# Section numbers of the graph hops read into registers for two groups at once, on SyncE and VectorE

## What is computed

```python
for _ in range(N_HOPS):            # 3
    h = agg[head]
    t = agg[tail]
    left = h @ q_w
    right = jnp.tanh(rel * t @ k_w)
    att = jnp.sum(left * right, axis=1)
    seg_max = jax.ops.segment_max(att, head, num_segments=n)
    e = jnp.exp(att - seg_max[head])
    seg_sum = jax.ops.segment_sum(e, head, num_segments=n)
    w = e / seg_sum[head]
    msg = w[:, None] * rel * t
    summed = jax.ops.segment_sum(msg, head, num_segments=n)
    agg = summed / jnp.maximum(cnt, 1.0)[:, None]
    norm = jnp.linalg.norm(agg, axis=1, keepdims=True)
    agg = agg / jnp.maximum(norm, 1e-12)
    out = out + agg + entity_emb
```

## Time and profile before

| | us |
|---|---|
| median of 3 timed runs | 11539.55 |
| lowest and highest | 11534.21, 11544.98 |
| span of the profiled execution | 11570.2 |
| PE busy, share of the span | 8077.2, 70% |
| DVE busy | 6642.3, 57% |
| POOL busy | 6401.1, 55% |
| ACT busy | 6199.6, 54% |

### The profile page before, as it was taken

One profiled execution on the slowest core, in us unless ns is written; L12 is line 12 of the kernel. 1 busy time (PEld: TensorE's weight loads), 2 busy tenths in 40 slices (PEclk: granted clock), 3 DMA queues, 4 the chain that ended last, 5 costly groups with the idle time before them and its releaser, 6 DMA issues. The chain is left out here.

```text
span 11570.2 us, 241070 instructions
## 1 busy us (share of the span) xinstructions
PE 8077.2 (70%) x47197; PEld 6146.6 (53%) x47197; DVE 6642.3 (57%) x27980; ACT 6199.6 (54%) x15908; POOL 6401.1 (55%) x6757
## 2 busy tenths in 40 slices
PE   2666666666688888888866666666666666666665
PEld 2444444444466666666645555555554555555554
DVE  4666666665555565655655555555554555555556
ACT  1666666666355555555545555555554555555554
POOL 4566666664455555555545555555545555555553
PEclk8776677767788999999978888888888888888887
DMA  2111111111455555555544444444434444444443
GB/s 68 43 43 43 43 43 42 43 43 41 123 176 176 177 176 176 177 175 176 176 124 139 138 138 138 137 139 136 138 118 134 136 138 137 138 136 136 137 136 112
DMA packets 1180950, 1401.16 MB, mean 121 GB/s; under 512 B 216215, under 2 KB 883640, under 8 KB 1180472
## 3 DMA queue, kind: packets, MB, share of 16 engines
q1 hardware_dynamic: 963734, 951.33, 25.8%
q0 software_dynamic: 216064, 444.28, 14.2%
q10 hardware_dynamic: 876, 2.56, 0.1%
HBM read 888.87 MB, written 183.76 MB: 93 GB/s over the span
## 5 line engine op out<-in xcount | busy, mean ns | idle before, releaser
L622 POOL DMA_INDIRECT tails<-node_rows,idx x4992 | 4715.4, 945 | 3803.9 <-remote 1610.6
L1798 DVE SCALAR_TENSOR_TENSOR acc<-acc,fade,banks 128x129 f32 x4992 | 1741.7, 349 | 2100.6 <-remote 1310.5
L1902 PE MATMUL banks<-rt,weight_t 128*128 128x129 f32 x9984 | 1674.8, 315 | 749.1 <-DVE acc L1798 724.3
L622 POOL DMA_INDIRECT l_rows<-in_x_dram,l_idx x1664 | 1591.9, 957 | 1075.1 <-issue 453.6
L1951 ACT ACTIVATE weight<-att,low 128x128 f32<-128x128 f32 x4992 | 1593.0, 391 | 1058.6 <-DVE low L1822 577.1
L1902 PEld LDWEIGHTS banks<-rt,weight_t 128*128 128x128 f32 x9984 | 1483.3, 223 | 849.8 <-issue 795.8
L1887 PE MATMUL banks<-rtt,k_sb 128*128 128x512 f32 x2496 | 1505.3, 685 | 533.8 <-issue 441.7
L1872 PE MATMUL banks<-right,window 128*128 128x128 f32 x9984 | 1567.3, 307 | 281.8 <-DVE tile_low L1814 163.4
L1814 DVE CUSTOM_DVE_ANT_0 att<-banks,agg 128x128 f32<-128x128 f32 x4992 | 1152.8, 287 | 982.6 <-remote 768.9
L1872 PEld LDWEIGHTS banks<-right,window 128*128 128x128 f32 x9984 | 1430.9, 221 | 358.3 <-DVE tile_low L1814 227.5
L1929 ACT ACTIVATE right<-banks 128x512 f32<-128x512 f32 x1248 | 730.5, 585 | 809.3 <-remote 639.2
(11 more groups left out here) (317 smaller groups left out, 9961.5 us busy)
## 6 DMA issues: line engine op xcount, KB each, us to landing
window<-qt SPq DMA_DIRECT2D x4992, 64.0 KB
agg<-pairs_kept SPq DMA_DIRECT2D x832, 384.0 KB
pairs_kept<-agg SPq DMA_DIRECT2D x416, 384.0 KB
rows_in<-tile_rows SPq DMA_DIRECT2D x208, 512.0 KB
tails<-node_rows,idx POOLq DMA_INDIRECT x4992
l_rows<-in_x_dram,l_idx POOLq DMA_INDIRECT x1664
node_rows<-agg SPq DMA_DIRECT2D x6, 1024.0 KB, 6.0
node_rows<-agg SPq DMA_DIRECT2D x3, 1088.0 KB, 8.2
```

Source lines behind the costliest of these rows:

```text
L622: e.indirect_dma_start(out=rows[:, g, t, :], out_offset=None, in_=of, in_offset=bass.IndirectOffsetOnAxis(ap=idx[:, b, first + t:first + t ...
L1798: e.scalar_tensor_tensor(to, to, fade[:, g2, t:t + 1], bank[b_acc + t // 2][:, t % 2 * WIDE:t % 2 * WIDE + WIDE], ALU.mult, ALU.add).then_ ...
L1902: mm = s.e.matmul(bank[b_acc + t // 2][:, t % 2 * WIDE:t % 2 * WIDE + WIDE], weight_t[:, s.slot(lag, 2), t, :], rt[:, s.slot(lag, RING), t ...
```

## The change

A new helper loads eight numbers at even steps and none at odd ones; a step takes the first or the last four of what is held. Both users in the hops are moved to it: SyncE's for the windows (lag 2) and VectorE's for the updates (lag 7). The calls now stand ahead of the test whether the step has a group at that lag. The first layer keeps the old helper.

```diff
+        def load_two_groups(s, e_type, at_section, most, lag, held):
+            if s.i % 2 == 0:
+                a = max(s.i - lag, 0)
+                b = min(s.i - lag + 2, z.slot_groups) if s.turn is None else s.i - lag + 2
+                if a < b:
+                    held[:] = load_sections(s, e_type, at_section, most, s.i - a, 0, (b - a) * GROUP)
+            if s.live(lag):
+                return held[-GROUP:] if (s.i % 2 or s.i == lag - 1) else held[:GROUP]
...
+                columns_held, wides_held = [], []
...
+                    q = load_two_groups(s, mybir.EngineType.SP, at_column, (z.sections - 1) * P, 2, columns_held)
                     if s.live(2):
                         g4 = s.slot(2, UNROLL)
-                        q = load_sections(s, mybir.EngineType.SP, at_column, (z.sections - 1) * P, 2)
                         s.wait_ge((s_att, done(2 + UNROLL)))
...
                 def update(s, lag):
+                    q = load_two_groups(s, mybir.EngineType.DVE, at_wide, (z.sections - 1) * WIDE, lag, wides_held)
                     if s.live(lag):
                         e, g2 = s.e, s.slot(lag, 2)
-                        q = load_sections(s, mybir.EngineType.DVE, at_wide, (z.sections - 1) * WIDE, lag)
                         s.wait_ge((s_acc, done(lag)), (s_taken, done(lag + 1, GROUP)))
```

## The result

| | before, us | after, us | ratio, 95% interval |
|---|---|---|---|
| median of 4 timed runs | 11538.52 | 11463.14 | 0.9935 (0.9921 to 0.9949) |
| span of the profiled execution | 11570.2 | 11460.8 | |

The change made the kernel 75 us faster, 0.65%. Forecast were 250 us, in a range that ended at 11080 and 11550. The time lies in the range and on the forecast side, but the gain is less than a third of the forecast.

A forecast was written before the change was run, and what follows sets the result against it. SyncE was taken to set the hops' pace; 0.43 - 0.03 = 0.40 us saved in two steps, 0.20 a group, times 1248 groups = 250 us. 11570 - 250 = 11320, less 30 for the timed median: 11290, range 11080 to 11550.

The forecast's parts named there:

- SyncE, even steps: SyncE's load of eight numbers instead of four in the hops: 0.03 us more; upper bound a 1402 ns load.
- What bounds the kernel: In the hops SyncE, waiting for nobody while others wait for its DMAs, sets the pace: 6.65 us a group.
- So no second engine cuts the gain short: In the hops, GpSimd's 5.0 and VectorE's 3.5 us a group stay under the 6.45 us left, so nothing limits the gain.
- SyncE, odd steps: In SyncE's odd hop steps one load and its address instruction go, with two joints: 0.43 us saved.
- VectorE: VectorE's loads before its updates in the hops: counted as nothing, with 0 to 100 us from hop 1 kept in the range.
- C: Rival: all engines' instruction total sets the pace; 1.0% fewer give about 120 us, 11420; chance 0.17.
- D: Rival: no change; SyncE's hold-ups are a matter of time or DMAs and fill the freed 0.20 us, 11540; chance 0.14.
- B: Rival: SyncE's hold-ups shrink with its fewer instructions, 470 us gained, 11070; chance 0.14.
- E: Rival: slower, SyncE's load of eight is dear; at 1402 ns it costs 420 us, 11960; chance 0.07.
- some 60 us if eight cost as much as two fours: By the Trainium skill's 200 ns a register, only the address instruction with its joint is saved, 0.09 us in two steps.
- What would show it: Signs in the profile after: fewer loads, medians near 330 and 400 ns, shorter hops, SyncE's own waits staying near nothing.
- A: The forecast case: SyncE's free duration comes back in the hops, 250 us gained, 11290; chance 0.48.

The follow-up runs named there:

- sp_no_load_again: Kernel before, but SyncE keeps the first group's four numbers for a whole hop, on a chip with hold-ups: 69 us faster, ratio 0.9950.
- vector_only: The change on VectorE alone against the kernel before; SyncE loads four numbers in every step as before: 11698.48 us, ratio 0.9999.
- sizes: Kernel before, but SyncE's load of section numbers has another size in each of 8 loop steps: 8906.64 us beside 8889.67.
- sp_no_load: Kernel before, but SyncE keeps the first group's four numbers for a whole hop, on the chip without hold-ups: 8887.8 us beside 8889.67, ratio 0.9998.

## Why the prediction was off

Two steps failed: the price of the load of eight, and the check for what is late next.

*SyncE, even steps*, 0.03 us more for eight numbers: measured 0.23 (525 against 297 ns). It was a line drawn through one number and four, and both lie on one step of the staircase. The upper bound, 1402 ns, held the value; the choice was by a slope where the nearest rows could not tell a slope from a step. With 0.23 the sum becomes 125 us, so this term is 125 of the 175 us by which the forecast was too high.

*What bounds the kernel.* "An engine that waits for nobody while others wait for its DMAs is the one that sets the pace" was right, but only for the next 70 to 100 us. SyncE was indeed the first limit with hold-ups: its part alone gave the whole gain, and ScalarE's wait for it fell by 731 us. The step that failed is the sentence "So no second engine cuts the gain short". It compared a group's 6.45 us with the gathers' 5.0 and VectorE's busy 3.5 us, that is with the work of engines that are not held up. Held up are their chains too, and the earlier trace rows showed VectorE's update standing 7.85 us, and the earlier trace rows 1310.5 us of such waits, more than ScalarE's 1033.5 for SyncE. The prediction names them and gives them no part in the sum. `sp_no_load_again` takes SyncE out, and they are still there, with 1617.1 us. It saves 0.5 us a group and gained 69 us, so 250 us were out of reach even with a load of eight of 330 ns. What should have been written is: a wait that no releaser is named for is not evidence for the engine that I suspect, and while it stands, the gain has a ceiling that I don't know.

*SyncE, odd steps*, 0.43 us for load and address instruction: 0.40 by the stretch from pair DMA to first window (0.21 for 0.61 us). Right.

*VectorE* counted as nothing: right for this change (`vector_only`, 0.9999), though the load of eight took 601 ns and not 400. "If SyncE's part were gone, this would be the next thing to show" was right too: with both kinds of loads gone 200 us came.

*The rivals.* C gave 11420 and was nearest by the number, by a mechanism that `sp_no_load_again` refutes. D's idea that the hold-ups fill what is freed describes the flat part of the line, though not by SyncE's own hold-ups. B, that hold-ups shrink with the instructions, is out: nothing came back beyond the free duration. E was right that the load of eight is dearer than its trend, and its point of turning at 0.73 us was not reached with 525 ns. The prediction also works out some 60 us if eight cost as much as two fours. That is close to the 75, partly by luck: the load is not quite so dear.

*What would show it* named 2727 us a hop for C and 2680 for A; 2761, 2714 and 2715 came. Its warning came true: "If these begin to grow instead, SyncE was not far from the real bound, and the gain ends there." SyncE's waits for the attention grew from 10.3 to 95.3 us.

## What to carry to other kernels

Before pricing a relief of the first limit, ask how far below it the second lies, and count waits whose releaser the trace can't name as a possible second limit, not as a symptom of the first. Where small register instructions of 33 to 56 ns have maxima of a microsecond, compare with another chip: here the same kernel took 23% less on one, and a gain found under hold-ups may be worth nothing without them. Load numbers into registers in fours: eight cost 1.8 times as much as four here, and two or three cost more than four. When an experiment removes instructions, measure what it frees instead of adding their durations up: four register instructions less ahead of the window DMAs freed nothing here.

## What the runs showed of the hardware

- A load of registers costs as if four numbers were one fetch and the remainder came one by one: 282, 476, 681, 302, 547, 741, 937, 537 ns for one to eight, 752 for twelve, on SyncE.
- The same program took 8890 us on one chip and 11540 to 11735 on the others. On the fast one the longest of 2346 register instructions in SyncE's wait helper (`sizes`) was 52 ns; in the trace before it was 1187 ns in hop 2 alone. What holds them up stays open. It was found on SyncE, VectorE and ScalarE (maxima of 1533, 1423 and 1393 ns in the wait helper, trace before), but not on TensorE's sequencer, whose 6918 register instructions of one kind there have a maximum of 100 ns, the same as in `sizes`. It isn't VectorE's loads, nor the number of instructions.
- With hold-ups, removing SyncE's loads alone gave 69 us, VectorE's alone 29, both 200.
- An indirect DMA of 128 rows kept GpSimd for 0.944 us, with 0.30 us to the next one: 1.25 us each where nothing was waited for (`sp_no_load`, hop 2).
